# Block numbers loaded four steps at a time, instead of sixteen, in the edge loops of a graph network kernel

## What is computed

```
L0:  agg = segment_sum(h[src], dst);  z = (1+eps)*h + agg;  two dense layers with batch norm
L1:  q, k, v = x@Wq, x@Wk, x@Wv;  sim = sum_d q[dst]*k[src]  (8 heads)
     attn = softmax of sim over the edges of one dst;  agg = segment_sum(attn * v[src], dst);  agg@Wo
L2:  x + z_in[in_deg] + z_out[out_deg] + gates + segment_sum(edge_attr@W_sum, src)
L3:  in  = segment_mean((x@W_in)[src], dst);  out = segment_mean((x@W_out)[dst], src)
     GRU cell of (in, out) and x
```

## Time and profile before

| | us |
|---|---|
| Time, median of 3 runs | 7838.82 (7830.95 to 7845.15) |
| The profiled execution's own time | 7829.5 |
| Its span, first to last instruction | 7827.8 |
| PE busy in it | 4856.9 (62%) |
| POOL busy | 4570.5 (58%) |
| DVE busy | 3195.1 (41%) |
| ACT busy | 549.0 (7%) |
| Mean granted TensorE clock | 0.75 of 2.4 GHz |

### The profile page before, as it was taken

One profiled execution on the slowest core, in us unless ns is written; L12 is line 12 of the kernel. 1 busy time (PEld: TensorE's weight loads), 2 busy tenths in 40 slices (PEclk: granted clock), 3 DMA queues, 4 the chain that ended last, 5 costly groups with the idle time before them and its releaser, 6 DMA issues. The chain is left out here.

```text
span 7827.8 us, 78801 instructions
## 1 busy us (share of the span) xinstructions
PE 4856.9 (62%) x16145; PEld 3002.0 (38%) x16145; DVE 3195.1 (41%) x7274; ACT 549.0 (7%) x1542; POOL 4570.5 (58%) x4631
## 2 busy tenths in 40 slices
PE   5666777638655556635555677655555566666668
PEld 2333333535322223224333575332222334444434
DVE  2222444538555555564444557511111123333318
ACT  0000000323000000010000001100000000000004
POOL 5666555656566666676655304666665566666650
PEclk8767666969667677667777899876666678878769
DMA  4443333322788888836666665322222233343345
GB/s 138 131 130 125 119 121 117 126 81 93 239 251 255 256 255 257 253 110 201 203 190 193 183 181 148 122 84 83 81 82 81 80 103 120 119 120 118 120 100 181
DMA packets 696672, 1164.04 MB, mean 149 GB/s; under 512 B 107648, under 2 KB 493805, under 8 KB 696134
## 3 DMA queue, kind: packets, MB, share of 16 engines
q0 software_dynamic: 224288, 633.55, 27.7%
q1 hardware_dynamic: 471864, 525.23, 21.0%
q10 hardware_dynamic: 110, 0.23, 0.0%
HBM read 870.83 MB, written 287.77 MB: 148 GB/s over the span
## 5 line engine op out<-in xcount | busy, mean ns | idle before, releaser
L2121 PE MATMUL l_sums<-big 128*128 (+1 forms) x3520 | 1297.7, 494 | 1028.1 <-issue 592.0
L189 DVE TENSOR_TENSOR big<-iota_row,dst_tab 128x512 f32<-128x512 f32 x660 | 458.2, 694 | 2572.6 <-PE l_sums L2121 963.4
L2121 PEld LDWEIGHTS l_sums<-big 128*128 128x128 f32 x3520 | 772.6, 240 | 1557.4 <-issue 1480.6
L1274 POOL DMA_INDIRECT bin_rows<-staging,place_tab x832 | 920.0, 1106 | 475.0 <-issue 240.1
L1160 POOL DMA_INDIRECT big<-kv_rows,idx_tab x880 | 834.4, 948 | 542.0 <-issue 243.9
L572 POOL DMA_INDIRECT big<-in_x,big x832 | 826.9, 994 | 517.3 <-SPq L148 265.2
L2078 POOL DMA_INDIRECT big<-x_rows,idx_tab x832 | 813.2, 977 | 529.5 <-SPq L148 281.8
L2078 POOL DMA_INDIRECT big<-x_rows,place_tab x880 | 887.2, 1008 | 392.4 <-issue 241.2
L1214 PE MATMUL es_q<-big 128*128 x1760 | 725.1, 540 | 472.8 <-issue 368.3
L606 PE MATMUL l_sums<-big 128*128 x1760 | 734.1, 554 | 326.6 <-issue 218.1
L1499 PE MATMUL ws_sums<-big 128*128 128x264 f32 x1760 | 534.5, 465 | 426.7 <-DVE big L1519 264.8
(11 more groups left out here) (296 smaller groups left out, 4920.3 us busy)
## 6 DMA issues: line engine op xcount, KB each, us to landing
v_edge<-big SPq DMA_DIRECT2D x880, 128.0 KB
big<-v_edge SPq DMA_DIRECT2D x440, 256.0 KB
bin_rows<-big SPq DMA_DIRECT2D x110, 520.0 KB
sims<-bin_rows SPq DMA_DIRECT2D x110, 520.0 KB
staging<-in_edges SPq DMA_DIRECT2D x104, 520.0 KB
gate_rows<-big SPq DMA_DIRECT2D x49, 512.0 KB
big<-gate_rows SPq DMA_DIRECT2D x49, 512.0 KB
big<-kv_rows,idx_tab POOLq DMA_INDIRECT x880
```

The lines of the kernel that those rows point to most:

```text
L189: return dve.tensor_tensor(out, rows, columns.unsqueeze(2).to_broadcast([P, QUAD, P]), ALU.is_equal)
L1274: pool.indirect_dma_start(k.bin_rows, bass.IndirectOffsetOnAxis(ap=k.place[:, c:c + 1], axis=0), k.staging[:, g % 2, j, :], None).then_inc ...
L2121: pe.matmul(sums[:, bank_of(node[u] + turn, D)], onehot[:, u % HALF, :], flat[:, bass.ds(at, D)], start=False, stop=True, skip_group_check ...
```

## The change

Only load_steps and its callers change. It loads QUAD = 4 numbers where it loaded 16, and TensorE calls it at each fourth step, with the registers indexed by step modulo 4. The loads of ACT (L120) and of SP (L129) keep their 16 values.

```diff
-def load_steps(nc, engine, row, it):
+def load_steps(nc, engine, row, quad):
     return nc.values_load_multi_w_load_instructions(
-        row[0:1, bass.ds(it * U, U)], engines=[engine.engine], min_val=1, max_val=NW,
+        row[0:1, bass.ds(quad * QUAD, QUAD)], engines=[engine.engine], min_val=1, max_val=NW,
@@ first_gather
-                if u == 0:
-                    node = load_steps(nc, pe, k.win, s // U)
+                if u % QUAD == 0:
+                    node = load_steps(nc, pe, k.win, s // QUAD)
-                chunk_ready(pe, s, node[u], s_here)
+                chunk_ready(pe, s, node[u % QUAD], s_here)
...
@@ edge_scores
-                block_at = load_steps(nc, pe, k.win, it)
                 for u in range(U):
                     s = it * U + u
+                    if u % QUAD == 0:
+                        block_at = load_steps(nc, pe, k.win, s // QUAD)
                     if u % QUAD == 0:
                         pe.wait_ge(s_hot, s + QUAD)
...
@@ weighted_sums
-                if s % U == 0:
-                    node = load_steps(nc, pe, k.win, s // U)
+                if s % QUAD == 0:
+                    node = load_steps(nc, pe, k.win, s // QUAD)
@@ attr_sums
-                if s % U == 0:
-                    node = load_steps(nc, pe, k.bin_win, s // U)
+                if s % QUAD == 0:
+                    node = load_steps(nc, pe, k.bin_win, s // QUAD)
@@ last_gathers
-                if u == 0:
-                    node = load_steps(nc, pe, k.bin_win if turn else k.win, t % STEPS // U)
+                if u % QUAD == 0:
+                    node = load_steps(nc, pe, k.bin_win if turn else k.win, t % STEPS // QUAD)
```

More of the change, by code:

```diff
@@ L598, in _ @@
                 u = s % U
-                if u == 0:
-                    node = load_steps(nc, pe, k.win, s // U)
-                chunk_ready(pe, s, node[u], s_here)
+                if u % QUAD == 0:
+                    node = load_steps(nc, pe, k.win, s // QUAD)
+                chunk_ready(pe, s, node[u % QUAD], s_here)
                 if s % QUAD == 0:
                     pe.wait_ge(s_hot, s + QUAD)
-                pe.wait_ge(s_free, node[u] & NODE_BITS)
-                pe.matmul(sums[:, bank_of(node[u], width)], onehot[:, u % HALF, :],
-                          flat[:, bass.ds(slot_of(s, node[u], D + 1), width)],
+                pe.wait_ge(s_free, node[u % QUAD] & NODE_BITS)
+                pe.matmul(sums[:, bank_of(node[u % QUAD], width)], onehot[:, u % HALF, :],
+                          flat[:, bass.ds(slot_of(s, node[u % QUAD], D + 1), width)],
                           start=False, stop=True, skip_group_check=True).then_inc(s_sum, 1)
@@ L1213, in _ @@
                     pe.wait_ge(s_prod, it * U + (U + u + 1 - 4))
-                    pe.matmul(qps[u % 4][:, 0:D], onehot[:, u % HALF, :], query[:, bass.ds(block_at[u] * D, D)],
+                    pe.matmul(qps[u % 4][:, 0:D], onehot[:, u % HALF, :], query[:, bass.ds(block_at[u % QUAD] * D, D)],
                               start=True, stop=True).then_inc(s_q, 1)
@@ L1497, in _ @@
                     pe.wait_ge(s_side, s + QUAD)
-                pe.wait_ge(s_free, node[s % U] & NODE_BITS)
-                pe.matmul(sums[:, bank_of(node[s % U], AW)], onehot[:, s % HALF, :], weighted[:, s % HALF, :],
+                pe.wait_ge(s_free, node[s % QUAD] & NODE_BITS)
+                pe.matmul(sums[:, bank_of(node[s % QUAD], AW)], onehot[:, s % HALF, :], weighted[:, s % HALF, :],
                           start=False, stop=True, skip_group_check=True).then_inc(s_sum, 1)
@@ L1575, in _ @@
                     pe.wait_ge(s_hot, s + QUAD)
-                pe.wait_ge(s_free, node[s % U] & NODE_BITS)
-                pe.matmul(sums[:, bank_of(node[s % U], EW)], onehot[:, s % HALF, :], ring[:, q % RING, r, 2:2 + EW],
+                pe.wait_ge(s_free, node[s % QUAD] & NODE_BITS)
+                pe.matmul(sums[:, bank_of(node[s % QUAD], EW)], onehot[:, s % HALF, :], ring[:, q % RING, r, 2:2 + EW],
                           start=False, stop=True, skip_group_check=True).then_inc(s_sum, 1)
@@ L2115, in _ @@
                 else:
-                    chunk_ready(pe, t, node[u], s_here)
-                at = u * D if turn else slot_of(t, node[u], D)
+                    chunk_ready(pe, t, node[u % QUAD], s_here)
+                at = u * D if turn else slot_of(t, node[u % QUAD], D)
                 if t % QUAD == 0:
                     pe.wait_ge(s_hot, t + QUAD)
-                pe.wait_ge(s_free, (node[u] & NODE_BITS) + turn * NW)
-                pe.matmul(sums[:, bank_of(node[u] + turn, D)], onehot[:, u % HALF, :], flat[:, bass.ds(at, D)],
+                pe.wait_ge(s_free, (node[u % QUAD] & NODE_BITS) + turn * NW)
+                pe.matmul(sums[:, bank_of(node[u % QUAD] + turn, D)], onehot[:, u % HALF, :], flat[:, bass.ds(at, D)],
                           start=False, stop=True, skip_group_check=True).then_inc(s_sum, 1)
```

## The result

| | Before | After |
|---|---|---|
| Time, median of 13 runs each in one comparison, us | 7834.32 (7799.45 to 7847.25) | 7858.29 (7829.17 to 7885.78) |
| Ratio after to before | | 1.0042, 95% interval 1.0026 to 1.0057 |
| Span of the profiled execution, us | 7827.8 | 7872.0 |

The change made the kernel slower by 0.42%, 33 us by the ratio. The forecast had the right sign but was four times too large: +131 us.

A forecast was written before the change was run, and what follows sets the result against it. No engine was full; the prediction took TensorE's sequencer to bind attr_sums and be late in relayed gathers, and data waits elsewhere. Terms 30 (attr_sums) + 87 (relayed stages) + 14 (others) = +131 us on 7838.8 gave 7970 us, range 7780 to 8220.

The forecast's parts named there:

- The reading of attr_sums: In attr_sums TensorE's sequencer binds and its loads are exposed almost whole, not DVE; the change adds 30 us.
- T4: Length of one load of four at line 113, taken as 0.45 us between bounds of 0.276 and 1.105.
- The low end's reasons: Line 113: differing load times on SP, ACT and PE and growth under DMA load suggest many small accesses, favouring 0.276 us.
- the 0.18 us added from ACT's slowest load: Fixed part of a load, from ACT's slowest being 184 ns above its median; added to 0.276 us.
- floor of about 600 ns: Trainium skill figure for any tensor_load, cited against so low a load price; by it the sum would be near +220 us.
- I pass on 0.7: In first_gather and the first pass of last_gathers, 0.7 of 96 us added sequencer time reaches the path: +67 us.
- The 20 us for the slow phases: Added for first_gather and last_gathers' first pass: 33 of 165 extra loads each fall where instructions cost about 0.7 us.
- Its own signs: Checks: load near 0.45 us, attr_sums +30 us, both relayed gather stages some +40 each, three others within 10 each.
- The three other stages: edge_scores, weighted_sums, second pass of last_gathers: loads stand ahead of waits, one tenth of 144 us charged, +14 us.
- all in the numbers: Rival at line 113: no fixed part, a load of four takes 0.276 us; +29 us, 7868 us, chance 0.20.
- Faster, by shorter pauses: Rival, mainly gather stages: PE's queued matmuls hide short pauses; -108 us, 7731 us, chance 0.20.
- The risk of the clock in attr_sums: More PE idle time might drop attr_sums to 1.2 GHz, making its 259 us of PE up to twice as long; held unlikely.

The follow-up runs named there:

- e2: Loads of four at each fourth step in first_gather and the first pass of last_gathers alone, against the kernel before, without slow phases: 6633.69 us, ratio 1.0002.
- e4: Loads of sixteen at each fourth step in all six passes, against the kernel before, without slow phases: 6805.35 us, ratio 1.0257.
- e11: Loads of sixteen at each fourth step in all six passes, against the kernel before, with slow phases: 7997.00 us, ratio 1.0220.
- e3: Loads of four in edge_scores, weighted_sums and the second pass of last_gathers alone, against the kernel before, without slow phases: 6630.69 us, ratio 0.9993.
- e12: Loads of four in edge_scores, weighted_sums and the second pass of last_gathers alone, against the kernel before, with slow phases: 7831.38 us, ratio 1.0012.
- e6: One number loaded at each step in all six passes, against the kernel before: 6867.25 us, ratio 1.0366.
- e7: Loads of 2, 12, 5, 8, 6 and 9 numbers in the six passes; one execution took 6604.32 us against 6627.60 of the kernel before.
- e8: Loads of sixteen at every second step in all six passes, against the kernel before: 10429.79 us, ratio 1.573.
- e5: The changed kernel again, without slow phases, against the kernel before: 6627.45 us, ratio 1.0000.
- e16: The kernel before, instruction for instruction, written with the new load_steps, without slow phases: ratio 1.0002 to the kernel before.

## Why the prediction was right or wrong

**The reading of attr_sums was right.** The idle time at a load is the load, not DVE, and the stage pays for it. With 0.332 in the place of 0.45 the term gives 55 x (4 x 0.282 - 1.05) = +4 us; measured +6, and +172 against 174 with loads of sixteen.

**The first step that failed is T4: 0.45 us taken, 0.332 measured.** It is most of the error. With the right T4 the whole sum would have been 4 + (31 + 20) + 7 = +62 us in the place of +131, and 33 were measured: 69 of the 98 us by which the forecast was too high come from this one term. The low end's reasons (three engines, three durations) were sound, but the 0.18 us added from ACT's slowest load was too much: what is fixed is 0.074 us. What the bounds could not show is that the cost goes by aligned groups of four. The changed kernel loads exactly one such group. The Trainium skill's floor of about 600 ns for a tensor_load (page "DMA: Bandwidth & Descriptors", section "Latency and other measured facts"), named as a reason against the change, doesn't hold for a row in SBUF: one number took 0.300 us. The Trainium skill's 200 ns for each register from HBM (page "Runtime: NRT & Kernel Launch", section "Instruction fetch mechanics") is near the 0.234 us that a number out of an aligned group took here from SBUF; loads of aligned fours take about a fourth of that for each number.

**The step whose mechanism failed is "I pass on 0.7".** The prediction read POOL's waits for SP L148 and TensorE's idle "issue" time as proof that TensorE's sequencer is late in the relayed stages, so that each added microsecond counts for 0.7. Without slow phases nothing was passed on (e2, e4). With them 385 us of added sequencer time in the two stages gave some 38 us in the profile of e11, and 960 us in five passes gave -1 us, give or take 25, in its times. TensorE is late there because its instructions are held up in the slow phases, as SP's are; between them it catches up (five steps in 2.89 us), and added loads of 1.1 us are absorbed. A wait for a late engine shows who is late. It doesn't show that more work makes it later, when what holds it is not its work.

**The 20 us for the slow phases** were put on both relayed stages at 0.7 us a load. The profiles have some 25 us in one of them, the times don't confirm it. It is near in size, but the reasoning (each load there costs what an instruction costs there) isn't shown, and first_gather speaks against it.

**Its own signs.** T4 fell between the 0.3 and 0.7 us that it set for itself. But the two gather stages should each have grown by some 40 us: first_gather was 19 us shorter, with 20 us less of POOL's wait, and the first pass of last_gathers 26 us longer.

**The three other stages** were given +14 us; e3 and e12 have -5 us (-11 to +1) and +9 us (-2 to +22). Neither is to be told from zero, as the rows on waits that end later said, nor is the second from +14.

**Of the rivals** "all in the numbers", +29 us and 7868, came out nearest, and that was luck, by two errors that offset each other: its T4 of 0.276 is too low (it made attr_sums 8 us shorter, where it became 6 longer), its coupling far too high. "Faster, by shorter pauses" didn't happen: the pauses that it wanted to save outside attr_sums weren't on the path. The risk of the clock in attr_sums didn't come true for the change (0.99 before and after).

**A version that is a little faster.** Every 8: 8 in attr_sums and sixteen elsewhere: 0.9987 (0.9978 to 0.9996) without slow phases; with them 0.9981 (0.9956 to 1.0006), which by itself isn't told from no change. attr_sums took 316 to 321 us in the four profiles with loads of eight there, and 324 to 331 in the eight with sixteen each 16 steps. Its two pauses of 0.54 us cost 2 us more than one of 1.05, and the second covers a wait that stood at step 8.

## What to carry to other kernels

Load registers in groups of four that begin at a multiple of four: the price here was 0.07 us a load and 0.26 us more for each group. Put a load where its engine waits anyway; at step 8 of attr_sums about half of a load of 0.59 us was hidden in that way. Before charging an engine's added time to a stage, find the pace of the stage (here one gather of POOL each 1.25 us) and what the engine needs below it; a large dose of the same thing, as in e11, measures that share better than any reading of waits.

## What the runs showed of the hardware

- A TENSOR_LOAD on TensorE's queue takes 0.074 us, plus 0.258 us for each whole group of four numbers, plus about 0.234 us for each number left over, if it begins at a multiple of four: 1, 2, 4, 8 and 16 numbers took 0.300, 0.537, 0.332, 0.591 and 1.105 us (e6, e7, after, before; 1 and 2 also from other places of the row, at the same price). 16 numbers that begin two off a multiple of four took 3.82 us (e8), which is 0.074 and sixteen times the 0.234 of a number left over.
- Slow phases. In some executions ordinary instructions of TensorE's and SP's sequencers take about 0.7 us in stretches of several us; in others not once (e5: 36 ns each time). In the kernel before it was 751 of TensorE's ALU_OP and FUSED_REGOPS records, 730 of them in the two relayed stages, and 178 of SP's ALU_OP records. The kernel before took about 7830 us in such executions and 6630 in the others, and one and the same chip showed both at different times. Nothing in the kernels decides it, and the cause is open. Nor are TensorE's slow instructions all of the difference: edge_scores has none of them and took 1366 us against 1098 (e16), weighted_sums has 5 and took 961 against 783, while attr_sums took 326 against 331. All readings of the earlier trace rows are readings of that state.
- The granted clock in attr_sums was 0.99 with pauses of 0.15 to 0.35 us, one after each four steps (after), 0.79 with loads of 1.1 us, one after each four (e4, e11), and 0.50 for the whole stage in e8 and with a load of 0.3 us after each step (e6):

```profile
3676.00:4235.00 559.00, 558.58 (x1760) 440.91 (x1759) 181.61 (x543) 26.07 (x98) 0.00 (x0) 0.50 0.39 104
```

Here PE counts as busy for all of its time and is at the lower of its two levels, 1.2 GHz. Two limits lie side by side there, and e6 can't tell them apart: the sequencer needs 0.25 + 0.30 + 0.06 = 0.61 us a step, and PE at the lower level needs 0.615 (two steps in 1.23 us in the lines of e8), of the measured 0.635.
